# A causal rotary attention stage: weights above the diagonal zeroed by GpSimd, value tails projected in the setup, split f16 outputs

## The chip, the cores and the metric

One core of a Trainium2 chip runs the whole program. The metric is the device time of one execution, in microseconds (us). TensorE is written PE (its weight loads PEld), VectorE DVE, ScalarE ACT, GpSimd POOL and the queue that only issues DMAs SP. Each engine takes its instructions in order and waits on semaphores for the others.

## What is computed

The reference is a network of several parts over x of shape 8 x 512 x 256: a modulated dense layer with a landmark attention, an LSTM, a small attention with picked heads, an adaptive layer, a rotary attention, an RNN and a mixture of experts. The change touches the rotary attention alone:

```python
def _L1_attn_ref(x, norm_weight, w_qkv, w_out, persist_mem):
    h = rms_norm(x, norm_weight)
    q, k, v = jnp.split(h @ w_qkv.T, 3, axis=-1)      # 16 heads of 64
    q = apply_rope(q); k = apply_rope(k)
    k = jnp.concatenate([pm, k], axis=2)              # 4 memory rows ahead of 512 tokens
    v = jnp.concatenate([pm, v], axis=2)
    scores = jnp.einsum('bhid,bhjd->bhij', q, k) * scale
    causal = j <= i + (kv_len - n)
    attn = jax.nn.softmax(jnp.where(causal, scores, finfo.min), axis=-1)
    out = jnp.einsum('bhij,bhjd->bhid', attn, v)
    return out.reshape(b, n, heads * dim_head) @ w_out.T
```

## The kernel before

The program is a row of stages, each with a barrier behind it. attention_stage first loads the weights and splits each f32 chunk of w_qkv into a high f16 part (ACT) and a low f16 part (DVE). It then calls attention_core, which handles one pair of heads of one batch at a time: 8 batches x 8 pairs make 64 pairs. A product of f32 numbers is made of three f16 products (high by high, high by low, low by high), accumulated in PSUM.

attention_core is a software pipeline written out by hand. Every engine has a function rope_slot(it, s) that issues its share of slot s, and the order inside it is the order of the queue. In slot s, PE projects q and k of pair s+2 and the values of pair s+2, makes the maxima's scores of pair s+1 (scores), the transposed scores of pair s (scores_T for key tiles 0, 1 and 2, and 3 in the next slot) and weights times values of pair s-1 (values). The keys are 4 memory rows and 512 tokens, so tile 4 (called QT in the code) has only 4 keys, the "tail". A fifth key tile needs a value tail of 4 rows, which value_tail projects for each pair with 6 products.

The steps of one pair that matter here:

- rotate (DVE) reads a projection, turn and sum_up (POOL) finish the rotation, high (ACT) makes its f16 part in QK, low (POOL) the rest. In POOL's rope_slot the k of pair s+1 has its low part at the start of slot s, q of s+2 at the end.
- scores_T (PE) writes st_ps. It ends in the mask products of L861, which add -1e30 above the diagonal: a 128x128 bf16 identity by the matrix att_after.
- exps (ACT) makes the weights twice, PH in f16 (L1043) and P32 in f32 (L1048); low_weights (DVE, L979) makes PL = P32 - PH. values (PE, L874) waits for p_low.
- normalise (DVE, L991 and L993), turn_outputs (PE, L879) and keep_outputs (ACT, L1061) leave the pair's output in ao, in f32. After every eighth pair outputs (PE, L886) multiplies ao by wo in f32, and add_outputs (DVE, L997) adds the result to XT. Such a slot is called an output slot below.

ACT's order at the start of a slot, and POOL's whole order, are:

```python
                if s>=1: exps(it,s-1,2); exps(it,s-1,3)
                if s>=-1: keep_tail(it,s+1); high(it,2*(s+1)+1)
...
                if s>=-1: low(it,2*(s+1)+1); split_tail(it,s+1)
                turn(it,q); sum_up(it,q)
                if new_batch(s): low_tokens(it,s+3)
                turn(it,k)
                low(it,q)
                sum_up(it,k)
```

Of the kernel before, what the change touches and what calls it, by code (L numbers as in the profile page):

```python
# [5 lines left out]
P=128  # L6
# [727 lines left out]
def attention_core(nc, XT, HT, c_):  # L734
# [25 lines left out]
    with ExitStack() as ctx:  # L760
# [17 lines left out]
        v_done,v_hi,v_low,tail_done,tail_kept,tail_low=[sem(n) for n in "v_done,v_hi,v_low,tail_done,tail_kept,tail_low".split(",")]  # L778
# [3 lines left out]
        pe_passed=sem("pe_passed")  # L782
# [8 lines left out]
        def _(pe):  # L791
# [14 lines left out]
            def values_of(it,n,out,t,rows):  # L806
# [81 lines left out]
            def first_tail(it,n):  # L888
                if n: pe.wait_ge(tail_kept,n)
                value_tail(it,n)  # L890
            def rope_slot(it,s):
# [3 lines left out]
                elif s>=-1: first_tail(it,s+1)  # L895
# [41 lines left out]
        def _(dve):  # L937
# [3 lines left out]
            nc.vector.memset(PH[:,:,:],0.0).then_inc(cleared,1)  # L941
            nc.vector.memset(PL[:,:,:],0.0).then_inc(cleared,1)
# [1230 lines left out]
```

## Time and profile before

| what | value |
| --- | --- |
| time of the kernel, median of 3 runs | 4001.85 us (4001.58 to 4002.23) |
| the profiled execution's own time | 3965.16 us |
| its span | 3963.4 us |
| busy over the span: PE, DVE, ACT, POOL | 83%, 57%, 43%, 30% |
| the rotary attention's setup | from 2148.6 us |
| its first PE product, and the last slot's end | 2189.7 us, about 3220 us |

Times of rows are microseconds from the span's start. A row of the timeline gives start, duration, engine, line, operation, the tiles written and read, the shape, how many instructions were merged, and in brackets how long the engine sat idle before it and what released it. A matmul's record is longer than the time that it keeps the engine, because matmuls are pipelined: the time that a group takes is read from its start to the start of the next group. An f32 matmul leaves two records.

### The profile page before, as it was taken

Reading aid. Unit: us, or ns where it says so; the run is one execution under the profiler, and the core shown is the slowest. Engines: PE = TensorE matmul, PEld = TensorE weight load, DVE = VectorE, ACT = ScalarE, POOL = GpSimd, SP = SyncE. Lnnn points to the kernel's source line nnn. Section 1 sums busy time; section 2 is a strip of 40 time slices with the busy share of each in tenths; the row PEclk is TensorE's granted clock in tenths of the full one; section 3 lists DMA queues with packets and bytes.
Section 4 is the critical chain, followed back from the end, with each engine's and each line's share of the span. In section 5 each row is a group of like instructions: output and inputs, shape, how many; then the busy total and the mean of one; then the engine's idle time right before and its main releaser. Section 6 shows DMA issues by size and latency. Waiting matters only on the chain. (4 is left out here: it accounts for less than half of the span.)

```text
span 3963.4 us, 142208 instructions
## 1 busy us (share of the span) xinstructions
PE 3296.6 (83%) x58228; PEld 2450.2 (62%) x58228; DVE 2267.9 (57%) x6676; ACT 1694.8 (43%) x5249; POOL 1201.1 (30%) x1587
## 2 busy tenths in 40 slices
PE   5667759898888888559984899999999979999682
PEld 4455448888888888535531466666666647777561
DVE  4437754444444444368865777877779755555333
ACT  0129633333333333247742455655556534444231
POOL 0012330000000000023320555554555554444432
PEclk8789955555555555589997899999999975555686
DMA  3001010000000000011101000000000010101335
GB/s 119 8 26 54 19 42 24 14 14 24 14 24 14 24 14 24 5 33 24 24 0 49 2 2 2 2 2 2 2 2 2 2 45 31 35 31 35 87 118 170
DMA packets 111064, 115.69 MB, mean 29 GB/s; under 512 B 53132, under 2 KB 94549, under 8 KB 110458
## 3 DMA queue, kind: packets, MB, share of 16 engines
q1 hardware_dynamic: 102762, 87.07, 7.8%
q0 software_dynamic: 7824, 21.46, 1.5%
q8 instruction: 396, 6.49, 0.7%
q14 instruction: 82, 0.67, 0.1%
HBM read 79.49 MB, written 29.00 MB: 27 GB/s over the span
## 5 line engine op out<-in xcount | busy, mean ns | idle before, releaser
L649 PE MATMUL banks<-hp,whp 128*128 128x8 f16 x24576 | 741.3, 168 | 117.5 <-DVE hp L716 117.5
L649 PEld LDWEIGHTS banks<-hp,whp 128*128 128x128 f16 x24576 | 697.7, 104 | 178.3 <-DVE hp L716 169.4
L682 ACT ACTIVATE ig<-banks 128x32 f32<-128x32 f32 x512 | 101.2, 198 | 577.5 <-PE banks L649 577.5
L1043 ACT ACTIVATE att_PH<-att_stp 128x1024 f16<-128x1024 f32 (+3 forms) x258 | 183.4, 711 | 374.0 <-PE att_stp L861 374.0
L711 DVE SCALAR_TENSOR_TENSOR carry<-ig 128x16 f32<-128x16 f32 x512 | 92.2, 180 | 425.3 <-ACT ig L682 425.3
L619 POOL COPY HT<-hist 128x128 f32 x64 | 21.2, 406 | 986.6 <-DVE hp L721 986.6
L1659 PEld LDWEIGHTS rnn_banks<-rnn_hp,rnn_whp 128*128 128x128 f16 x6144 | 251.8, 108 | 102.3 <-ACT rnn_hp L1717 70.9
L1659 PE MATMUL rnn_banks<-rnn_hp,rnn_whp 128*128 128x8 f16 x6144 | 285.5, 171 | 35.3 <-ACT rnn_hp L1717 11.2
L1108 POOL TENSOR_TENSOR att_QK<-att_rot,att_QK 128x512 f16<-128x512 f32 x133 | 173.6, 1305 | 338.5 <-ACT att_QK L1035 338.5
L627 PE MATMUL banks<-xs,wxp 128*128 128x64 f16 x3168 | 264.9, 241 | 0.0
L979 DVE TENSOR_TENSOR att_PL<-att_P,att_PH 128x1024 f16<-128x1024 f32 (+3 forms) x257 | 235.1, 934 | 18.1 <-ACT att_P L1049 16.5
L804 PE MATMUL att_pj<-att_hT,att_w 128*128 128x512 f16 x804 | 199.2, 384 | 49.9 <-POOL att_hT L1116 48.4
L962 DVE TENSOR_REDUCE att_mx<-att_sp 128x2 f32<-128x264 f32 (+3 forms) x263 | 210.6, 822 | 30.3 <-PE att_sp L835 30.3
L1811 DVE TENSOR_TENSOR rnn_hp<-rnn_hist,rnn_hp 128x16 f16<-128x16 f32 x512 | 100.3, 196 | 204.0 <-ACT rnn_hist L1718 199.1
L1717 ACT ACTIVATE rnn_hp<-rnn_banks 128x16 f16<-128x16 f32 x512 | 94.2, 184 | 268.9 <-PE rnn_banks L1659 266.9
L1099 POOL TENSOR_TENSOR att_ab<-att_ab,att_rope 128x512 f32<-128x512 f32 x134 | 169.2, 1263 | 113.5 <-DVE att_ab L952 113.5
L627 PEld LDWEIGHTS banks<-xs,wxp 128*128 128x128 f16 x3168 | 195.7, 127 | 0.0
L1048 ACT ACTIVATE att_P<-att_stp 128x1024 f32<-128x1024 f32 (+3 forms) x258 | 180.5, 700 | 4.2 <-DVE att_PL L979 4.2
L874 PE MATMUL att_acc<-att_V,att_PH 128*128 128x65 f16 (+1 forms) x3584 | 179.8, 193 | 0.0
L874 PE MATMUL att_acc<-att_V,att_PL 128*128 128x65 f16 x1792 | 174.9, 192 | 0.0
L1103 POOL TENSOR_TENSOR att_rot<-att_ab 128x512 f32<-128x512 f32 x134 | 170.2, 1271 | 14.8
L716 DVE TENSOR_TENSOR hp<-og,tc 128x16 f16<-128x16 f32 x512 | 90.0, 176 | 144.3 <-ACT tc L688 144.3
(572 smaller groups left out, 7910.8 us busy)
## 6 DMA issues: line engine op xcount, KB each, us to landing
gen_w<-in_L_cond_W_dram SPq DMA_DIRECT2D x32, 512.0 KB, 4.2
exp_xt<-expert_rows_scratch SPq DMA_DIRECT2D x80, 129.0 KB, 2.3
edge_cb<-cols_scratch SPq DMA_DIRECT2D x16, 512.0 KB, 3.7
XT<-expert_found_scratch SPq DMA_DIRECT2D x16, 512.0 KB, 5.1
mod_xn<-in_x_dram SPq DMA_DIRECT2D x8, 512.0 KB, 3.7
XT<-in_xT_dram SPq DMA_DIRECT2D x1, 4096.0 KB
out_dram<-exp_ob SPq DMA_DIRECT2D x64, 64.0 KB, 2.2
attw_st<-in_L_attn_w_qkvT_dram SPq DMA_DIRECT2D x6, 512.0 KB, 4.4
```

Of the source, the lines that this page charges most:

```text
L627: last=nc.tensor.matmul(out, wxp[:,wpart,k,col:col+128], xs[:,st,xpart,k,steps], start=False,stop=False,skip_group_check=True)
L649: last=nc.tensor.matmul(out, whp[:,wpart,k,col:col+128], hp[:,k,hpart], start=False,stop=True,skip_group_check=True)
L804: last=nc.tensor.matmul(pj[:,:],c_.w_of(n)[:,wpart,k,col:col+P],h_of(n)[:,xpart,k,PM:PM+T],start=(i==0),stop=(i==5)); i+=1
L874: last=nc.tensor.matmul(out[:,0:wide],p[:,h,at:at+P],V[:,n%4,tt,part,h,0:wide],start=(tt==0 and a==0 and p is PH and part==0),stop=(tt==(R ...
L962: i=nc.vector.tensor_reduce(out=mx[:,:,qt:qt+1],in_=s_ps[:,:,at:at+w_],axis=X_AX,op=ALU.max); at+=w_
L979: i=nc.vector.tensor_tensor(PL[:,:,at:at+w_],P32[:,t%2,:,0:w_],PH[:,:,at:at+w_],ALU.subtract)
L1043: nc.scalar.activation(PH[:,:,at:at+w_],st_ps[:,:,0:w_],ACT.Exp,scale=DH**-0.5)
L1048: i=nc.scalar.activation(P32[:,t%2,:,0:w_],st_ps[:,:,0:w_],ACT.Exp,scale=DH**-0.5)
L1099: nc.gpsimd.tensor_tensor(ab[:,1],ab[:,1],c_.tab[:,1],ALU.mult).then_inc(turned,1)
L1103: nc.gpsimd.tensor_tensor(rot_of(j),ab[:,0],ab[:,1],ALU.add).then_inc(summed,1)
L1108: nc.gpsimd.tensor_tensor(dst[:,1],rot_of(j),dst[:,0],ALU.subtract).then_inc(lo,1)
L1659: last=nc.tensor.matmul(pre(st,par)[:,u,j], whp[:,wpart,k,u*P:u*P+P], hp[:,k,hpart], start=False,stop=True,skip_group_check=True)
```

## The change

- The mask products L861 leave scores_T. In their place POOL's new mask_weights sets the weights above the diagonal to zero, in PH and PL together, which now lie in one tile PHL: one affine_select over 128 partitions x 4 x 128 f16 for each key tile (t), and one more of 4 x 4 x 4 for the tail. values waits for its semaphore masked instead of p_low. POOL's slot order gets four such steps: for pair s-1 and t=1 first, then the low part of k, then t=2 and t=3, and at the slot's end pair s and t=0.
- value_tail, keep_tail and split_tail leave the loop. The setup projects the last 4 tokens of all batches at once, splits them and stores them in DRAM; SP fetches the 4 rows of a pair into V, in the loop.
- The memory values (pmv) enter with one product of 36 rows instead of two of 4.
- ao and wo are kept as two f16 parts. keep_outputs writes the high part, the new low_outputs (DVE) the low part, and outputs makes three f16 products for each f32 one. The value bank vo is free again after low_outputs.
- PE projects the values of pair s+2 after the third group of scores instead of before it.
- The setup loads all six chunks of w_qkv without waiting for a buffer; ACT and DVE also split wo there.

The diff, cut to what the text speaks of:

```diff
-        PH=sb("PH",[P,2,PCOLS],F16); PL=sb("PL",[P,2,PCOLS],F16); P32=sb("P32",[P,2,2,PM+T])
-        ao=sb("ao",[P,NP_,T]); o32=sb("o32",[P,QT,2,DH]); inv=sb("inv",[P,2,QT])
-        tail=sb("tail",[PM,2,DH]) if rope else None
+        PHL=sb("PHL",[P,2,2,PCOLS],F16); PH=PHL[:,0]; PL=PHL[:,1]; P32=sb("P32",[P,2,2,PM+T])
+        ao=sb("ao",[P,NP_,2,T],F16) if rope else sb("ao",[P,NP_,T]); o32=sb("o32",[P,QT,2,DH]); inv=sb("inv",[P,2,QT])
         mx=sb("mx",[P,2,5]); mparts=sb("mparts",[P,QT,P],BF16)
...
                 if rope and t==0:
-                    for part in range(2):
-                        last=nc.tensor.matmul(out,c_.identh[:,:],c_.pmv[:,n%NP_,part],start=False,stop=(part==1),skip_group_check=True)
+                    last=nc.tensor.matmul(out,c_.identh[:,:],c_.pmv[:,n%NP_],start=False,stop=True,skip_group_check=True)
...
-                elif n>2: pe.wait_ge(o_kept,it*S+n-2)
+                elif n>2: pe.wait_ge(o_low if rope else o_kept,it*S+n-2)
...
-            def value_tail(it,n):
-                values_of(it,n,st_ps[0:PM,0,T-P:T],QT,PM).then_inc(tail_done,1)
...
-                    if rope: pe.wait_ge(tail_kept,it*S+n+2)
...
-                if rope and t==QT-1: value_tail(it,n+2)
...
-                        for h in range(2): last=nc.tensor.matmul(st_ps[0:rows,h,at:at+w_],k_[head(h),kpart,tt*P:tt*P+rows],q[head(h),qpart,q0:T],start=False,stop=(i==2 and not rope),skip_group_check=True)
-                    if rope:
-                        d0=PM if tt==0 else 0; d1=PM if tt==QT else P
-                        for h in range(2): last=nc.tensor.matmul(st_ps[0:rows,h,at:at+d1-d0],c_.after[:,0:rows],c_.identb[:,d0:d1],start=False,stop=True,skip_group_check=True)
+                        for h in range(2): last=nc.tensor.matmul(st_ps[0:rows,h,at:at+w_],k_[head(h),kpart,tt*P:tt*P+rows],q[head(h),qpart,q0:T],start=False,stop=(i==2),skip_group_check=True)
                 last.then_inc(st_done,1)
...
-                pe.wait_ge(p_low,it*S*QT+n*QT+t+1)
+                pe.wait_ge(masked if rope else p_low,it*S*QT+n*QT+t+1)
...
-                if rope and t==QT-1: pe.wait_ge(tail_low,it*S+n+1)
+                if rope and t==QT-1: pe.wait_ge(tail_in[n%4],16*(it*(S//4)+n//4+1))
...
-                    last=nc.tensor.matmul((pj,vo)[m][:,:],c_.wo[:,q,m*P:(m+1)*P],ao[:,q,:],start=(q==0),stop=(q==NP_-1))
+                    if rope:
+                        for i,(wpart,opart) in enumerate(((0,0),(1,0),(0,1))):
+                            last=nc.tensor.matmul((pj,vo)[m][:,:],c_.wo[:,wpart,q,m*P:(m+1)*P],ao[:,q,opart,:],start=(q==0 and i==0),stop=(q==NP_-1 and i==2))
+                    else: last=nc.tensor.matmul((pj,vo)[m][:,:],c_.wo[:,q,m*P:(m+1)*P],ao[:,q,:],start=(q==0),stop=(q==NP_-1))
...
+                if s>=-1: scores(it,s+1,2)
                 if not after_outputs(s+2): project_values(it,s+2)
-                if s>=-1: scores(it,s+1,2)
...
+            def low_outputs(it,n):
+                dve.wait_ge(o_kept,it*S+n+1)
+                nc.vector.tensor_tensor(ao[:,n%NP_,1,:],vo[:,:],ao[:,n%NP_,0,:],ALU.subtract).then_inc(o_low,1)
...
                 if s>=-1: maxima(it,s+1,1)
+                if s>=1: low_outputs(it,s-1)
                 if out: add_outputs(it,s-1,0)
...
+                def tail_rows(b,n):
+                    rows=c_.tails[bass.ds(b,1),:,n%NP_].rearrange("a m part h d -> (a m) part h d")
+                    sp.dma_start(V[0:PM,n%4,QT,:,:,0:DH],rows).then_inc(tail_in[n%4],16)
+                for n in range(4): tail_rows(0,n)
+                with loop(nc,sp,NB//BPI) as it:
+                    for n in range(4,S+4):
+                        sp.wait_ge(pv_done,it*S*QT+(n-3)*QT)
+                        tail_rows(batch(it,n),n)
+                for i in range(4): sp.wait_ge(tail_in[i],16*(NB*NP_//4+1))
...
-            def keep_tail(it,n):
-                act.wait_ge(tail_done,it*S+n+1)
-                if n: act.wait_ge(tail_low,it*S+n)
-                nc.scalar.activation(V[0:PM,n%4,QT,0,:,0:DH],by_head(st_ps[0:PM,0,T-P:T]),ACT.Copy)
-                nc.scalar.activation(tail[:,:,:],by_head(st_ps[0:PM,0,T-P:T]),ACT.Copy).then_inc(tail_kept,1)
...
-                if s>=-1: keep_tail(it,s+1); high(it,2*(s+1)+1)
+                if s>=-1: high(it,2*(s+1)+1)
...
-            def split_tail(it,n):
...
+            def mask_weights(it,n,t):
+                pool.wait_ge(p_low,it*S*QT+n*QT+t+1)
+                pool.sem_inc(pool_passed,1)
+                for tt in ([t,QT] if t==QT-1 else [t]):
+                    d0=PM if tt==0 else 0; wide=(PM if tt==QT else P)-d0; rows=PM if tt==QT else P; at=written(tt)
+                    w=PHL[0:rows,:,:,at:at+wide].rearrange("p a h q -> p (a h) q")
+                    i=nc.gpsimd.affine_select(out=w,in_=w,compare_op=ALU.is_ge,fill=0.0,base=d0,pattern=[[0,4],[1,wide]],channel_multiplier=-1)
+                i.then_inc(masked,1)
...
-                if s>=-1: low(it,2*(s+1)+1); split_tail(it,s+1)
+                if s>=1: mask_weights(it,s-1,1)
+                if s>=-1: low(it,2*(s+1)+1)
+                if s>=1: mask_weights(it,s-1,2); mask_weights(it,s-1,3)
                 turn(it,q); sum_up(it,q)
                 if new_batch(s): low_tokens(it,s+3)
                 turn(it,k)
                 low(it,q)
                 sum_up(it,k)
+                if s>=0: mask_weights(it,s,0)
             def flat_slot(it,s):
...
+        wo=sb("wo",[P,2,PAIRS,D],F16); tab=sb("rope",[P,2,T]); pmk=sb("pmk",[P,PAIRS,2,PM],F16); pmv=sb("pmv",[PMR,PAIRS,P],F16)
...
+                for c in ORDER:
+                    sp.dma_start(st[:,c],w_qkvT[:,c*512:(c+1)*512].rearrange("(k p) n -> p k n",p=P)).then_inc(ld[c],16)
+                sp.dma_start(pk32[:,:,:],pmT).then_inc(ldk,16)
+                for r in (0,32): sp.dma_start(pv32[r:r+PM,:,:],pmV.rearrange("m n h d -> m n (h d)")).then_inc(ldk,16)
+                sp.dma_start(wo32[:,:,:],w_outT.rearrange("(a p) n -> p a n",p=P)).then_inc(wo_in,16)
+                sp.dma_start(tab[:,:,:],rope).then_inc(tab_in,16)
+                sp.wait_ge(kept_hi,2)
+                rows=tails.rearrange("b m n part h d -> (b m) n part (h d)")
+                sp.dma_start(rows[:,:,0],kept[:,0].rearrange("p (n e) -> p n e",e=P)).then_inc(written,16)
+                sp.wait_ge(kept_lo,2)
+                sp.dma_start(rows[:,:,1],kept[:,1].rearrange("p (n e) -> p n e",e=P)).then_inc(written,16)
+                sp.wait_ge(tab_in,16)
...
+                pe.wait_ge(last_tokens,3)
+                for j in range(2):
+                    pe.wait_ge(lo,j+1)
+                    i=0; col=2*INNER_+j*512
+                    for k in range(2):
+                        for wpart,xpart in ((0,0),(1,0),(0,1)):
+                            m=nc.tensor.matmul(ps[:,j],last[:,xpart,k],w[:,wpart,k,col:col+512],start=(i==0),stop=(i==5)); i+=1
+                    m.then_inc(projected,1)
...
+                    if i in (2,3):
+                        act.wait_ge(projected,i-1)
+                        nc.scalar.activation(kept[:,0,(i-2)*512:(i-1)*512],ps[:,i-2],ACT.Copy).then_inc(kept_hi,1)
+                act.wait_ge(wo_in,16)
+                nc.scalar.activation(wo[:,0],wo32[:,:,:],ACT.Copy).then_inc(wo_hi,1)
...
+                        at=slice((i-2)*512,(i-1)*512)
+                        nc.vector.tensor_tensor(kept[:,1,at],ps[:,i-2],kept[:,0,at],ALU.subtract).then_inc(kept_lo,1)
...
+                dve.wait_ge(wo_hi,1)
+                nc.vector.tensor_tensor(wo[:,1],wo32[:,:,:],wo[:,0],ALU.subtract).then_inc(pmh,1)
```

## Rows read from the trace of the kernel before

**Rows 1.** Windows: engines' busy us in one slot, TensorE's granted clock, DMA

```profile
2601.86:2615.71 13.85, 13.85 (x213) 8.96 (x210) 11.26 (x21) 8.12 (x18) 6.74 (x6) 1.00 0.01 2
```

**Rows 2.** One line's instructions, L991: duration min/median/max, first and last start

```profile
L991 DVE RECIPROCAL att_inv<-att_acc x64: 207/208/209, 2229.4 to 3198.9; 128x8 f32<-128x8 f32 x64
```

**Rows 3.** Timeline of PE, one ordinary slot

```profile
2603.26 0.39 PE L856 MATMUL att_stp<-att_mT,att_ones 64*128 64x512 bf16 x2
...
2604.23 0.28 PE L861 MATMUL att_stp<-att_identb,att_after 128*128 128x124 bf16 x2
2604.45 0.23 PE L832 MATMUL att_sp<-att_QK 64*128 64x132 f16 x2
...
2606.47 0.60 PE L879 MATMUL att_vo<-ident,att_o 128*128 128x128 f32 x4
...
2612.97 0.50 PE L810 MATMUL att_stp<-att_w,att_hT 128*4 128x128 f16 x6
2613.40 0.23 PE L856 MATMUL att_stp<-att_mT,att_ones 64*128 64x132 bf16 x2
...
2614.25 0.23 PE L874 MATMUL att_acc<-att_V,att_PH 128*128 128x65 f16 x2
```

**Rows 4.** Timeline of ACT, the same slot

```profile
2610.23 0.63 ACT L1035 ACTIVATE att_QK<-att_rot 128x512 f16<-128x512 f32 x1
...
2614.36 0.39 ACT L1043 ACTIVATE att_PH<-att_stp 128x264 f16<-128x264 f32 x1 [1.47 <-PE att_stp L861]
...
2615.44 0.61 ACT L1035 ACTIVATE att_QK<-att_rot 128x512 f16<-128x512 f32 x1
```

**Rows 5.** Timeline of POOL, the same slot

```profile
2610.94 1.42 POOL L1108 TENSOR_TENSOR att_QK<-att_rot,att_QK 128x512 f16<-128x512 f32 x1 [1.58 <-ACT att_QK L1035]
2612.43 1.26 POOL L1103 TENSOR_TENSOR att_rot<-att_ab 128x512 f32<-128x512 f32 x1
2616.13 1.16 POOL L1108 TENSOR_TENSOR att_QK<-att_rot,att_QK 128x512 f16<-128x512 f32 x1 [2.44 <-ACT att_QK L1035]
```

**Rows 6.** Timeline of DVE, the same slot

```profile
2608.85 2.50 DVE L979 TENSOR_TENSOR att_PL<-att_P,att_PH 128x1024 f16<-128x1024 f32 x2
...
2612.52 1.20 DVE L969 TENSOR_TENSOR att_mx<-att_mx 128x2 f32<-128x2 f32 x1
```

**Rows 7.** Timeline of POOL and DVE in the LSTM stage

```profile
1203.73 0.40 POOL L606 COPY xf<-XT 128x128 f32 x1
1203.74 0.42 DVE L719 TENSOR_TENSOR hist<-og,tc 128x16 f32<-128x16 f32 x1
```

**Rows 8.** One line's instructions, L719: duration ns min/median/max

```profile
L719 DVE TENSOR_TENSOR hist<-og,tc x512: 167/168/420, 552.9 to 1646.6; 128x16 f32<-128x16 f32 x171
```

**Rows 9.** Groups by form: busy us, mean ns, idle us before

```profile
L1187 POOL TENSOR_SCALAR_AFFINE_SELECT att_after<-att_after 128x128 bf16<-128x128 bf16 x1 | 0.3, 292 | 0.2 <-POOL att_after L1185 0.2
L2048 POOL TENSOR_SCALAR_AFFINE_SELECT adapt_mask<-adapt_mask 64x8 f32<-64x8 f32 x1 | 0.2, 185 | 0.1
L1244 POOL IOTA pick_heads_i<- 128x512 int32 x1 | 0.7, 671 | 0.0
...
L979 DVE TENSOR_TENSOR att_PL<-att_P,att_PH 128x520 f16<-128x520 f32 x64 | 44.8, 701 | 1.1 <-issue 1.1
L986 DVE TENSOR_TENSOR att_V<-att_vo,att_V 128x512 f16<-128x512 f32 x66 | 45.0, 682 | 2.1 <-ACT att_V L1053 1.1
```

**Rows 10.** Timeline of PE in an output slot

```profile
2337.27 3.65 PE L886 MATMUL att_vo<-att_ao,att_wo 128*128 128x512 f32 x8
2340.76 3.60 PE L886 MATMUL att_pj<-att_ao,att_wo 128*128 128x512 f32 x8
```

**Rows 11.** Timeline of the setup, SP and DVE

```profile
2148.61 0.38 SPq L1155 DMA_DIRECT2D attw_st<-in_L_attn_w_qkvT_dram  x1
...
2177.37 1.23 DVE L1179 TENSOR_TENSOR att_w<-attw_st,att_w 128x1024 f16<-128x1024 f32 x1 [1.50 <-ACT att_w L1166]
```

**Rows 12.** DMA view from 2140 to 2200 us, 40 slices of 1.5 us

```profile
GB/s 0 0 0 0 0 5 55 348 361 331 371 265 37 3 0 0 60 343 277 19 61 289 164 184 0 0 5 0 0 0 0 0 0 0 0 0 0 0 0 0
```

More of the change, by code:

```diff
@@ L777, in attention_core @@
         h_hi,h_ready,cleared,proj,evac,turned,summed,hi,lo,pm_kept=[sem(n) for n in "h_hi,h_ready,cleared,proj,evac,turned,summed,hi,lo,pm_kept".split(",")]
-        v_done,v_hi,v_low,tail_done,tail_kept,tail_low=[sem(n) for n in "v_done,v_hi,v_low,tail_done,tail_kept,tail_low".split(",")]
+        v_done,v_hi,v_low,o_low=[sem(n) for n in "v_done,v_hi,v_low,o_low".split(",")]
+        tail_in=[sem(f"tail_in{i}") for i in range(4)] if rope else None
         s_done,maxed,m_step,m_ready,m_turned,m_copied=[sem(n) for n in "s_done,maxed,m_step,m_ready,m_turned,m_copied".split(",")]
@@ L872, in values @@
                             at=weights_at(tt,a); out=acc[:,h,a*(DH+1):(a+1)*(DH+1)]
-                            for p,part,wide in ((PH,0,DH+1),(PH,1,DH),(PL,0,DH+1)):
-                                last=nc.tensor.matmul(out[:,0:wide],p[:,h,at:at+P],V[:,n%4,tt,part,h,0:wide],start=(tt==0 and a==0 and p is PH and part==0),stop=(tt==(ROWS-1) and p is PL),skip_group_check=True)
+                            for low,part,wide in ((0,0,DH+1),(0,1,DH),(1,0,DH+1)):
+                                last=nc.tensor.matmul(out[:,0:wide],PHL[:,low,h,at:at+P],V[:,n%4,tt,part,h,0:wide],start=(tt==0 and a==0 and low==0 and part==0),stop=(tt==(ROWS-1) and low==1),skip_group_check=True)
                 last.then_inc(pv_done,1)
@@ L1025, in _ @@
             slots(rope_slot if rope else flat_slot,dve)
-        if not rope: c_.select(nc,block,ctx,hi)
+        if rope:
+            @block.sync
+            def _(sp):
+                sp.wait_ge(cleared,6)
+                def tail_rows(b,n):
[7 more added lines that the diff above has]
+                for i in range(4): sp.wait_ge(tail_in[i],16*(NB*NP_//4+1))
+        else: c_.select(nc,block,ctx,hi)
         @block.scalar
@@ L1133, in _, with attention_stage @@
             slots(rope_slot if rope else flat_slot,pool)
-def attention_stage(nc, XT, HT, w_qkvT, w_outT, pmT, pmV, rope, ident):
+def attention_stage(nc, XT, HT, w_qkvT, w_outT, pmT, pmV, rope, ident, tails):
     with ExitStack() as ctx:
@@ L1162, in _ @@
             @block.scalar
             def _(act):
-                for c in range(NCH):
-                    act.wait_ge(ld[c%2],16*(c//2+1))
-                    nc.scalar.activation(w[:,0,:,c*512:(c+1)*512],st[:,c%2],ACT.Copy).then_inc(hi,1)
+                for i,c in enumerate(ORDER):
+                    act.wait_ge(ld[c],16)
+                    nc.scalar.activation(w[:,0,:,c*512:(c+1)*512],st[:,c],ACT.Copy).then_inc(hi,1)
+                    if i in (2,3):
+                        act.wait_ge(projected,i-1)
+                        nc.scalar.activation(kept[:,0,(i-2)*512:(i-1)*512],ps[:,i-2],ACT.Copy).then_inc(kept_hi,1)
@@ new lines, in _ @@
+                dve.wait_ge(last_tokens,1)
+                nc.vector.tensor_copy(last[:,0],low_last[:,:,:]).then_inc(last_tokens,1)
+                dve.wait_ge(last_tokens,2)
+                nc.vector.tensor_tensor(last[:,1],low_last[:,:,:],last[:,0],ALU.subtract).then_inc(last_tokens,1)
+                nc.vector.tensor_copy(identb[:,:],ident[:,:]).then_inc(pmh,1)
+                nc.vector.memset(pmv[:,:,:],0.0).then_inc(pmh,1)
+                for i,c in enumerate(ORDER):
+                    dve.wait_ge(hi,i+1)
+                    nc.vector.tensor_tensor(w[:,1,:,c*512:(c+1)*512],st[:,c],w[:,0,:,c*512:(c+1)*512],ALU.subtract).then_inc(lo,1)
+                    if i in (2,3):
+                        dve.wait_ge(kept_hi,i-1)
+                        at=slice((i-2)*512,(i-1)*512)
+                        nc.vector.tensor_tensor(kept[:,1,at],ps[:,i-2],kept[:,0,at],ALU.subtract).then_inc(kept_lo,1)
@@ L1188, in _ @@
                 step(nc.gpsimd.memset(ones[:,:],1.0))
+                step(nc.gpsimd.memset(identh[:,:],0.0))
+                for r in (0,32):
+                    step(nc.gpsimd.affine_select(out=identh[r:r+PM,:],in_=identh[r:r+PM,:],compare_op=ALU.not_equal,fill=1.0,base=0,pattern=[[-1,P]],channel_multiplier=1))
         c=Core(); c.pairs=PAIRS; c.rope=True; c.pm=PM; c.w=w; c.wo=wo; c.tab=tab; c.pmk=pmk; c.pmv=pmv; c.after=after; c.ones=ones; c.identb=identb; c.identh=identh; c.ident=ident; c.name='att'
+        c.tails=tails
         c.batch_per_turn=BPI_ATT; c.h_buffers=BPI_ATT; c.w_of=lambda n: w
```

62 lines of the change are left out of this document (26 added, 36 removed).

## The prediction

> **What bounds the kernel now.** The windows by stage come first, since the change touches one stage: the rotary attention, 2148.6 to about 3220 us. In an ordinary slot PE is busy for all of 13.85 us at a granted clock of 1.00 (2.4 GHz), DVE for 11.26, ACT for 8.12 and POOL for 6.74 [rows 1]. So PE sets the slot. L991 runs once a slot; its 64 starts lie 969.5 us apart [rows 2], 15.39 us a slot. With 56 intervals of 13.85 and 7 across an output slot, that makes 27.7 us for each of the latter. Then come the timelines of the same slot, engine by engine: the reader is to see where PE is in its order when the other engines deliver. POOL is idle half the time, but it does the low part of k late: scores_T of tile 3 ends at 2614.25 on PE [rows 3], ACT makes the last weights from 2614.36 and only then the high part of k, from 2615.44 [rows 4], and POOL can take the low part from 2616.13, for 1.16 us [rows 5]. Today nobody on PE waits for that before the next slot.
>
> **The change, part by part.**
>
> *PE gives back 1.6 us a slot.* The value tail took 2612.97 to 2613.40, 0.43. scores_T of tile 0 took 2603.26 to 2604.45, 1.19, of which 0.22 is its mask [rows 3]; without the mask PE stays on 64-row products and need not switch to 128 rows and back, for which I take 0.10, so 0.32 go. scores_T of tile 3 with its tail took 0.85 (2613.40 to 2614.25): two masks and one switch go, about 0.43. Six products of 128 columns took 0.43 in the tail, 0.07 each; the masks of tiles 1 and 2 thus give 0.14 each, the merged memory product 0.07, and moving the value projection saves a switch, 0.10. The sum is 1.6. By itself that would be a slot of 12.25.
>
> *The outputs give back 3.7 us per output slot.* Eight f32 records, four products, took 3.49 and 3.53 us [rows 10], 0.88 each; 16 are 14.1 us. Three f16 products of 512 columns replace each, at four times the 0.054 of 128 columns net of issue, 0.217: 10.4 us. 8 x 3.7 = 30 us, less what the new waits take back (below).
>
> *low_outputs* costs DVE what low_values of the same shape costs, 0.68 [rows 9]. DVE would have 11.9 us a slot, under the 12.25, so it is no bound by its sum. It delays low_weights of tiles 0 and 1 behind it by 0.6. The value projection now waits for it and for the maxima that it was moved past, about 0.75 us of PE in a slot. Both are hidden if the slot is set elsewhere, as I hold it is.
>
> *The masks on POOL.* No row shows this size. The same operation takes 0.292 us for 128 elements a partition and 0.185 for 8 [rows 9]: 0.89 ns an element, 0.63 us for 512. The bounds are 0.29 (as if four rows cost one) and 1.17 (four times the small one); a generator of 512 elements took 0.67 [rows 9], near the first figure, so I take 0.63, 0.19 for the tail, and 0.07 to 0.10 between two POOL instructions that wait. POOL's sum rises from 6.74 to about 9 us: not a bound either. The place in the queue is what costs. In a slot POOL now does, without a pause: low of q, sum of k, mask 0, mask 1, low of k, mask 2, mask 3. values of tiles 2 and 3 wait for the last two; behind them on PE stand scores_T of tile 0, the scores and the projection of k, whose end starts the rotation that leads to low of q and sum of k again. That is a ring, and I add it up from the end of PE's projection of k:
>
> - to the end of POOL's sum of k: before, 2606.47 [rows 3] to 2613.69 (2612.43 + 1.26 [rows 5]), 7.2. low_weights of tile 1 ended there at 2611.35 [rows 6], and low of q ended 1.0 later. low_outputs puts that back by 0.6; the 0.4 that low_weights of tile 0 now loses to POOL goes. New: 7.4.
> - masks 0 and 1, low of k, masks 2 and 3 with the tail: 4 x 0.63 + 0.19 + 1.16, and five gaps: 4.3. low of k could not start before 8.75 in this count: scores_T of tile 3 ends at 7.2 (PE's 7.8 of before, less 1.35, plus the 0.75), and 1.88 of ACT follow it [rows 3 to 5], less 0.3 for the two tail copies. The first two masks end at 8.9, so the two conditions nearly meet.
> - DVE's operations that fall into this stretch and share POOL's port: 1.1 (next paragraph).
> - values of tile 3, 18 of the products of L874: 0.55.
> - scores_T of tile 0, the first scores and the projection of k: 2603.26 to 2606.47 less 0.32, 2.9.
>
> Sum 16.25; I forecast 16.2 us for an ordinary interval, 2.35 above today's 13.85. PE is then idle for some 4 us of it.
>
> *The port.* DVE's L969, two columns from SBUF, took 1.20 us beginning 0.09 after POOL's sum of k, and ended with it [rows 5, 6]; POOL's low of q took 1.42 instead of 1.16 while a low_weights ran. Whether an operation of POOL with one input does the same, the LSTM stage shows: a POOL copy from 1203.73 for 0.40 stretched a DVE operation with two SBUF inputs to 0.42, where the median is 0.168 [rows 7, 8]. So I take it that affine_select, which reads SBUF too, excludes DVE's two-input operations. L975, low_weights of tile 2 (0.70 [rows 9]) and of tile 3 (about 0.4, plus its tail) must run between the masks, and mask 3 depends on them: 1.1 net of overlap.
>
> The Trainium skill ("SBUF — State Buffer", Who interferes with whom) says the same in general: a DVE instruction with two SBUF inputs contends with a GpSimd instruction that reads SBUF, and the second to issue waits for the whole of the first. By it the ring is 16.2, without it 15.1; for affine_select itself no run here shows it. The skill's "GPSIMD Engine Reference" (Elementwise — side-by-side cycle accounting) gives for a tight loop about 1.8 cycles an element, 0.77 us for 512; by this estimate the ring would be 0.56 longer than with my slope from [rows 9].
>
> *What else waits.* Behind mask 3 on POOL stand turn and sum of q; DVE's rotation of k and ACT's high of q need them. They end at 12.8 + 2.7 = 15.5 in my count, before the projection of k ends (16.2). The fetch of a tail is issued three slots ahead and hidden; if that cover went, some 4 us would be added a slot, as a small load takes.
>
> *Output intervals.* They save 1.6 + 3.7, and give back the wait for low_outputs (1.2, nothing covers it there) and the stall before tiles 2 and 3 (about 1.8, since the value projection after an output slot covers 1.7 of it): 2.3 each, 18 us in 8.
>
> *Setup.* The last low part ends at 2178.6 today [rows 11]. The queue reached 331 to 371 GB/s when it had work [rows 12]. All 4.75 MB then land 13.6 us after 2150.5, the chunk of wo at about 2163. ACT needs two pieces of 1.06 for it and DVE two of 1.23; DVE's own list (six chunks 7.4, memory rows about 3, tails 1.5, wo 2.5) ends near 2169.5. The tails' two stores lie under that. Gain 9 us (5 to 12).
>
> **Sum.** 56 x 2.35 = +132, outputs -18, setup -9: +105 us. The profiled execution took 3965.16 us for a span of 3963.4; the median of the runs is 36.7 us above it, and I add the difference to the median: 4001.85 + 105 = 4107.
>
> **Rivals.**
> - *The masks don't lose the port.* Ring 15.1, output intervals 3.3 saved: 56 x 1.25 - 26 - 9 = +35, 4037. For it: no row shows affine_select beside DVE. Against: [rows 7].
> - *Masks at a bound.* At 0.29 each and no port loss low of k waits for ACT, the interval is 14.35 and the sum 28 - 28 - 9, -9: 3993. At 1.17 each the ring is 18.4 and the time about 4230.
> - *Faster: the masks are short enough to fit in POOL's idle time.* With no cost for them the chain through low of k alone gives 13.9 and -35, 3967. The sides change at an interval of 14.5, a mask of about 0.35 without port loss. If some slack that I don't see lets PE remain the bound, with slots of 12.3 to 13, the sum is near -110, 3890. For it: POOL is half idle and PE full [rows 1]. Against: POOL's idle time lies before low of k [rows 5], where masks 2 and 3 can't be.
> - *The clock.* PE would be busy for three quarters of a slot; if its granted clock fell to 0.5, PE's part of the ring doubles, several us a slot, over 4300. Its pauses are under 3 us, so I give it little.
>
> **How the numbers follow.** My forecast (intervals 15.6 to 16.8, 4070 to 4150) has 0.50; no port loss or cheaper masks but still slower 0.25; dearer masks or the clock 0.07; a small result within 0.2% 0.05; faster 0.13. 0.2% is 8 us, about what a measurement of this kernel can tell from no change. The range 4015 to 4150 takes in the case without port loss and leaves out the faster cases and the dear masks.
>
> **What the profile after would show.** L991 at intervals of 16.2; PE idle before L874's tiles 2 and 3, released by POOL's PHL, 2 to 3 us a slot; 320 affine_selects, 256 of about 0.63; DVE's L975 and small low_weights lengthened beside them; DVE's new subtraction at 0.68; L886's work down to 10.4 us an output slot; the setup done near 2169; a clock of 1.00. An interval under 14.5, or PE waiting for DVE instead of POOL, would make the prediction wrong, and so would a mask far from 0.63.

## The result, and the profile after

The changed kernel took 4072.97 us (median of 4 runs, 4070.12 to 4076.09) against 4002.04 us: a ratio of 1.0175, 95% interval 1.0158 to 1.0193. It is 71 us slower, where 105 were forecast; 4073 lies in the range of 4015 to 4150.

The two spans differ by more, 4068.4 - 3963.4 = 105 us. A second profile of the kernel before (experiment e0 below) has a span of 4003.2 us and the same ordinary slot. Against that one the difference of 65 us falls apart as in the table. The expert stage runs there from the first load of exp_xt to the start of its last write-back (L1932 before, L1982 after):

| part | before, second profile | after | difference |
| --- | --- | --- | --- |
| all ahead of the attention's setup | 2152.8 | 2154.8 | +2.0 |
| setup, first DMA issue to the core's first memset | 30.7 | 21.6 | -9.1 |
| attention core, to the RNN's first instruction | 1045.4 | 1123.8 | +78.4 |
| RNN and dispatch | 497.9 | 493.5 | -4.4 |
| expert stage | 218.5 | 217.1 | -1.4 |
| from there to the end of the span | 57.9 | 57.6 | -0.3 |

The page after, its busy line and slices:

```profile
PE 3230.3 (79%) x57260; PEld 2395.4 (59%) x57260; DVE 2396.8 (59%) x6745; ACT 1675.2 (41%) x5120; POOL 1387.5 (34%) x1845
...
PE   5667758888888888389895888888888879999572
...
PEclk8789955555555555599997999999999975555686
```

Each slice is 102 us. The attention fills slices 22 to 31, counted from 0: PE falls there from 9 tenths or more to 8, and the clock stays at 9 tenths or more. The windows view of one ordinary slot comes next (stretch, its length, busy us of PE, PEld, DVE, ACT and POOL, the granted clock, the DMA share and GB/s), and then the line of the reciprocal, L981 now, which answers [rows 2]:

```profile
2631.02:2646.61 15.59, 13.02 (x191) 8.14 (x191) 14.53 (x23) 8.14 (x16) 10.95 (x12) 1.00 0.00 1
```

```profile
L981 DVE RECIPROCAL att_inv<-att_acc x64: 207/208/209, 2226.8 to 3279.3; 128x8 f32<-128x8 f32 x64
```

The ordinary interval is 15.59 us instead of 13.85. 63 intervals make 1052.5 us; read from the single starts, the 56 ordinary ones are 15.61 on average and the seven across an output slot 25.5 instead of 27.7. The granted clock in the slot is 1.00. PE in this slot, the groups around its waits (they answer [rows 3]):

```profile
2633.80 0.60 PE L871 MATMUL att_vo<-ident,att_o 128*128 128x128 f32 x4
...
2636.31 0.39 PE L829 MATMUL att_sp<-att_QK 64*128 64x512 f16 x2 [0.42 <-DVE att_mx L953]
...
2641.85 1.62 PE L866 MATMUL att_acc<-att_V,att_PHL 128*128 128x65 f16 x48 [0.70 <-POOL att_PHL L1121]
2643.31 0.39 PE L841 MATMUL att_sp<-att_identb,att_mparts 128*128 128x128 bf16 x4
2644.88 0.72 PE L866 MATMUL att_acc<-att_V,att_PHL 128*128 128x65 f16 x18 [1.19 <-POOL att_PHL L1121]
2645.86 0.72 PE L866 MATMUL att_acc<-att_V,att_PHL 128*128 128x65 f16 x18 [0.26 <-POOL att_PHL L1121]
2646.51 0.39 PE L851 MATMUL att_stp<-att_mT,att_ones 64*128 64x512 bf16 x2
```

The reader is to see the brackets: before values of tile 0 (0.70 us), of tile 2 (1.19) and of tile 3 (0.26) PE sat idle until POOL's L1121, the affine_select. With the 0.42 for DVE's maxima that is all of its idle time in the slot. POOL and DVE at the same time (they answer [rows 5] and [rows 6]):

```profile
2638.05 1.82 POOL L1109 TENSOR_TENSOR att_QK<-att_rot,att_QK 128x512 f16<-128x512 f32 x1 [1.38 <-ACT att_QK L1042]
2639.95 1.26 POOL L1104 TENSOR_TENSOR att_rot<-att_ab 128x512 f32<-128x512 f32 x1
2641.17 1.22 POOL L1121 TENSOR_SCALAR_AFFINE_SELECT att_PHL<-att_PHL 128x496 f16<-128x496 f16 x2
2642.65 1.39 POOL L1109 TENSOR_TENSOR att_QK<-att_rot,att_QK 128x512 f16<-128x512 f32 x1 [0.27 <-ACT att_QK L1042]
2644.00 0.83 POOL L1121 TENSOR_SCALAR_AFFINE_SELECT att_PHL<-att_PHL 128x512 f16<-128x512 f16 x1
2645.00 0.80 POOL L1121 TENSOR_SCALAR_AFFINE_SELECT att_PHL<-att_PHL 128x512 f16<-128x512 f16 x2 [0.18 <-DVE att_PHL L972]
```

```profile
2640.03 1.21 DVE L959 TENSOR_TENSOR att_mx<-att_mx 128x2 f32<-128x2 f32 x1
2641.27 0.57 DVE L963 TENSOR_SCALAR att_mparts<-att_mx 128x8 bf16<-128x8 f32 x1
2641.87 0.57 DVE L965 SCALAR_TENSOR_TENSOR att_mparts<-att_mx,att_mparts 128x8 bf16<-128x8 f32 x1
2642.34 1.99 DVE L969 TENSOR_TENSOR att_PHL<-att_P,att_PHL 128x520 f16<-128x520 f32 x2
2644.25 0.58 DVE L972 TENSOR_TENSOR att_PHL<-att_P,att_PHL 4x8 f16<-4x8 f32 x1
```

POOL runs the seven steps of the ring with hardly a pause, masks 0 and 1 merged in one row. DVE's small operations are held up beside them, by the port as I read it: L963 and L965 take 0.57 each. The groups by form from 2400 to 3100 us give their mean, before (L973, L975) and then after:

```profile
L975 DVE SCALAR_TENSOR_TENSOR att_mparts<-att_mx,att_mparts 128x8 bf16<-128x8 f32 x45 | 8.8, 195 | 1.6
L973 DVE TENSOR_SCALAR att_mparts<-att_mx 128x8 bf16<-128x8 f32 x45 | 8.3, 185 | 1.6
```

```profile
L1121 POOL TENSOR_SCALAR_AFFINE_SELECT att_PHL<-att_PHL 128x496 f16<-128x496 f16 x42 | 26.2, 623 | 41.4 <-DVE att_PHL L969 41.4
...
L969 DVE TENSOR_TENSOR att_PHL<-att_P,att_PHL 128x264 f16<-128x264 f32 x42 | 53.3, 1269 | 0.0
...
L972 DVE TENSOR_TENSOR att_PHL<-att_P,att_PHL 4x8 f16<-4x8 f32 x42 | 24.4, 582 | 0.0
L963 DVE TENSOR_SCALAR att_mparts<-att_mx 128x8 bf16<-128x8 f32 x42 | 23.8, 567 | 1.5
L965 DVE SCALAR_TENSOR_TENSOR att_mparts<-att_mx,att_mparts 128x8 bf16<-128x8 f32 x42 | 22.7, 542 | 1.4
```

### The profile page after: what moved, and what is told of

It reads as the page before. It is cut to its first block and busy times, and to the rows that moved or that the text cites. A ratio compares the mean times of both kernels' runs of the same rounds, so it can differ in the third digit from the quotient of the medians.

```text
span 4068.4 us, 141073 instructions
## 1 busy us (share of the span) xinstructions
PE 3230.3 (79%) x57260; PEld 2395.4 (59%) x57260; DVE 2396.8 (59%) x6745; ACT 1675.2 (41%) x5120; POOL 1387.5 (34%) x1845
## 5 line engine op out<-in xcount | busy, mean ns | idle before, releaser
L1050 ACT ACTIVATE att_PHL<-att_stp 128x1024 f16<-128x1024 f32 (+3 forms) x258 | 183.2, 710 | 419.6 <-PE att_stp L853 419.6
L1709 PE MATMUL rnn_banks<-rnn_hp,rnn_whp 128*128 128x8 f16 x6144 | 286.1, 171 | 37.8 <-ACT rnn_hp L1767 13.9
L866 PE MATMUL att_acc<-att_V,att_PHL 128*128 128x65 f16 (+1 forms) x5376 | 195.5, 193 | 131.2 <-POOL att_PHL L1121 131.2
L866 PEld LDWEIGHTS att_acc<-att_V,att_PHL 128*128 128x128 f16 x5376 | 172.8, 97 | 155.7 <-POOL att_PHL L1121 147.9
L969 DVE TENSOR_TENSOR att_PHL<-att_P,att_PHL 128x1024 f16<-128x1024 f32 (+3 forms) x257 | 260.9, 1053 | 0.5 <-issue 0.2
L1109 POOL TENSOR_TENSOR att_QK<-att_rot,att_QK 128x512 f16<-128x512 f32 x133 | 204.6, 1539 | 109.6 <-ACT att_QK L1042 109.6
L1121 POOL TENSOR_SCALAR_AFFINE_SELECT att_PHL<-att_PHL 128x512 f16<-128x512 f16 (+2 forms) x321 | 181.7, 582 | 92.3 <-DVE att_PHL L969 81.1
L1104 POOL TENSOR_TENSOR att_rot<-att_ab 128x512 f32<-128x512 f32 x134 | 170.3, 1271 | 15.1
```

The costliest lines, as they stand in the source:

```text
L866: last=nc.tensor.matmul(out[:,0:wide],PHL[:,low,h,at:at+P],V[:,n%4,tt,part,h,0:wide],start=(tt==0 and a==0 and low==0 and part==0),stop=(t ...
L969: i=nc.vector.tensor_tensor(PL[:,:,at:at+w_],P32[:,t%2,:,0:w_],PH[:,:,at:at+w_],ALU.subtract)
L1050: nc.scalar.activation(PH[:,:,at:at+w_],st_ps[:,:,0:w_],ACT.Exp,scale=DH**-0.5)
L1104: nc.gpsimd.tensor_tensor(rot_of(j),ab[:,0],ab[:,1],ALU.add).then_inc(summed,1)
L1109: nc.gpsimd.tensor_tensor(dst[:,1],rot_of(j),dst[:,0],ALU.subtract).then_inc(lo,1)
L1121: i=nc.gpsimd.affine_select(out=w,in_=w,compare_op=ALU.is_ge,fill=0.0,base=d0,pattern=[[0,4],[1,wide]],channel_multiplier=-1)
```

## The experiments

All but e0 start from the changed kernel. "Interval" is the distance of two ordinary starts of the reciprocal in the experiment's own profile. "Ratio" is to the kernel before, timed beside that experiment, with its 95% interval in brackets.

### e0: the kernel before, profiled again

> The kernel before once more, unchanged, for a second profile of it. The profiled execution of before took 3965 us, while its timed runs took 4001 to 4006 (now 3994 to 4008 in 11 runs), and the expert stage lasted 192 us in it, but 217 to 223 us in the profiles of the changed kernel and of the four experiments so far. Theory: that one execution had a short expert stage by chance, and a second profile shows 215 to 223 us there, the same ordinary interval of 13.85 us, and a span near 4000. Rival: the expert stage of the kernel before is really shorter, 192 us again, and the change lengthened it by 25 us from afar.

Span 4003.2 us, time 4004.97 (a single run); interval 13.85; expert stage 218.5 us. The profiles of all eleven changed versions have 214 to 223 us there too. The first profile's 192 us in that stage was an accident of that execution, and the change is not charged with it. The interval of 13.85, on which the forecast stood, is the same in both.

### e1: the low part of k behind the masks

```diff
-                if s>=1: mask_weights(it,s-1,1)
-                if s>=-1: low(it,2*(s+1)+1)
-                if s>=1: mask_weights(it,s-1,2); mask_weights(it,s-1,3)
+                if s>=1: mask_weights(it,s-1,1); mask_weights(it,s-1,2); mask_weights(it,s-1,3)
+                if s>=-1: low(it,2*(s+1)+1)
```

> The changed kernel with one line of POOL's order moved: masks 1, 2 and 3 first, then the low part of k. Theory (the ring through POOL's queue): values of tiles 2 and 3 no longer wait behind the 1.2 to 1.4 us of the low part of k and behind ACT's high part, so the ordinary interval falls from 15.59 us to about 14.8 (masks 0 and 1 still come late) and the time by about 45 us, to 4028, ratio to the kernel before 1.006. Rival (the masks' own durations and their port set the slot, wherever they stand): interval stays at 15.3 to 15.6, time over 4055.

Time 4016.39, ratio 1.0035 (1.0024 to 1.0045); interval 14.77. POOL's timeline, one slot:

```profile
2630.75 1.27 POOL L1104 TENSOR_TENSOR att_rot<-att_ab 128x512 f32<-128x512 f32 x1
2631.98 1.22 POOL L1121 TENSOR_SCALAR_AFFINE_SELECT att_PHL<-att_PHL 128x496 f16<-128x496 f16 x2
2634.00 0.68 POOL L1121 TENSOR_SCALAR_AFFINE_SELECT att_PHL<-att_PHL 128x512 f16<-128x512 f16 x1 [0.80 <-DVE att_PHL L969]
2634.85 0.81 POOL L1121 TENSOR_SCALAR_AFFINE_SELECT att_PHL<-att_PHL 128x512 f16<-128x512 f16 x2 [0.17 <-DVE att_PHL L972]
2635.64 1.15 POOL L1109 TENSOR_TENSOR att_QK<-att_rot,att_QK 128x512 f16<-128x512 f32 x1
```

From the end of the sum of k to the end of mask 3 it is now 3.6 us (2632.02 to 2635.66) instead of 4.6. Two swapped lines give back 57 of the 71 us, 12 more than expected; the intervals across output slots fell too, from 25.5 to 24.7. What is left in the ring shows in the bracket of mask 2: it waits 0.80 for DVE's L969, which comes late because L963 and L965 ahead of it took 0.57 and 0.56 beside masks 0 and 1, instead of 0.19 and 0.20.

### e2: no masking at all

The three lines that call mask_weights are gone, and values waits for p_low in place of masked.

> The changed kernel without any masking: no operation on POOL and no product on PE, values waits for the low part again, so weights above the diagonal stay in the output. Theory: with the ring gone PE sets the slot, 12.25 us of its own work and about 0.75 us of waits for the maxima and low_outputs: interval 12.9 to 13.1, time about 4002 + 56 x (13.0 - 13.85) - 8 x 3.9 - 10 = 3913, ratio 0.978. Rival (the vo bank, held until low_outputs, or DVE's sum is what lengthens the slot): interval 14.5 or more, ratio above 1.00.

Time 3932.7, ratio 0.9819 (0.980 to 0.9839); interval 13.02, some at 14.0. One slot's windows:

```profile
2617.20:2630.22 13.02, 12.60 (x191) 8.08 (x191) 12.40 (x23) 8.14 (x17) 8.03 (x6) 1.00 0.01 3
```

PE sets the slot again, though not by much: it is busy for 12.60 of the 13.02, DVE for 12.40. So the masks on POOL cost 2.6 us a slot, and neither the vo bank nor DVE's sum does. The time came out 20 us above the expected 3913; 13 of it are the ordinary intervals, 13.24 on average over all 56.

### e3: masks that only write

```diff
-                    i=nc.gpsimd.affine_select(out=w,in_=w,compare_op=ALU.is_ge,fill=0.0,base=d0,pattern=[[0,4],[1,wide]],channel_multiplier=-1)
+                    i=nc.gpsimd.memset(w,1.0)
```

> The changed kernel with each affine_select replaced by a memset of the same columns to 1.0, so that the masked blocks are all ones in the output: POOL keeps its place and its waits, but only writes. Theory with the port (reading POOL work excludes DVE's two-input work): memset of 512 takes 0.52 instead of 0.62 and DVE's L965 and L969 are no longer stretched beside it, the interval falls to about 14.9, of which 0.4 is the shorter operation. Rival (the port costs nothing here): 15.2.

Time 4027.02, ratio 1.0055 (1.0036 to 1.0074); interval 14.90. The groups by form show what the port does:

```profile
L963 DVE TENSOR_SCALAR att_mparts<-att_mx 128x8 bf16<-128x8 f32 x44 | 36.9, 839 | 1.5
...
L965 DVE SCALAR_TENSOR_TENSOR att_mparts<-att_mx,att_mparts 128x8 bf16<-128x8 f32 x44 | 10.3, 234 | 1.5
L972 DVE TENSOR_TENSOR att_PHL<-att_P,att_PHL 4x8 f16<-4x8 f32 x44 | 6.5, 148 | 0.0
```

L972, with two SBUF inputs, is short again, 0.148 instead of 0.582, and it runs inside the memset of mask 2. L965 is short as well, 0.234 instead of 0.542, but shows nothing: L963 ahead of it, with one input, is held until both memsets have ended, and L965 has none beside it. POOL and then DVE in one slot:

```profile
2628.39 0.98 POOL L1121 MEMSET att_PHL<- 128x496 f16 x2
2631.21 1.14 POOL L1121 MEMSET att_PHL<- 128x512 f16 x3
...
2628.51 0.90 DVE L963 TENSOR_SCALAR att_mparts<-att_mx 128x8 bf16<-128x8 f32 x1
2629.45 0.20 DVE L965 SCALAR_TENSOR_TENSOR att_mparts<-att_mx,att_mparts 128x8 bf16<-128x8 f32 x1
...
2631.48 0.15 DVE L972 TENSOR_TENSOR att_PHL<-att_P,att_PHL 4x8 f16<-4x8 f32 x1
```

So a POOL operation that only writes leaves the two-input L972 alone, and one that reads doesn't. L963 and L965 together take as long as in the changed kernel, 1.10 against 1.14. The memset itself took 0.524 us, 0.1 less than the select; four of them are 0.4 of the 0.69 us that the interval fell, and the port's share is at most the other 0.3.

### e4: the mask products back on PE

As e2, with the products of L861 restored behind the three products of scores_T; tails in the setup, split outputs and the later value projection stay.

> The changed kernel with the mask products on PE again and nothing masked on POOL; tails in the setup, split outputs and the later value projection stay. Theory: PE sets the slot with 13.85 less 0.43 for the tail and 0.06 for the memory product, plus up to 0.5 of waits for the maxima and low_outputs: interval 13.4 to 13.85, outputs save about 2.5 us eight times, setup 10: time 3945 to 3972, ratio 0.986 to 0.993. Rival (the split outputs or the late values are what made the kernel slower): ratio above 1.00.

Time 3966.4, ratio 0.991 (0.9891 to 0.993); interval 13.80. The rest of the change is a gain of 36 us; masking by POOL alone turned it into a loss. The two kernels differ by 107 us.

### e5: values projected ahead of the third scores again

On top of e4:

```diff
-                if s>=-1: scores(it,s+1,2)
                 if not after_outputs(s+2): project_values(it,s+2)
+                if s>=-1: scores(it,s+1,2)
```

> As e4_products_back (mask products on PE, no masks on POOL), and the value projection ahead of the third group of scores again. Theory: PE then waits at the value projection for low_outputs, about 1.0 us, instead of 0.4 and 0.2 at the scores and the projection, so the interval is 13.8 to 14.1, no shorter than the 13.80 of e4. Rival (moving the projection alone made e4 miss its 13.4): interval 13.4.

Time 3995.33, ratio 0.9979 (0.997 to 0.9988); interval 14.34, above the 13.8 to 14.1 of the theory. PE now waits at the value projection for low_outputs, 0.8 to 1.0 us a slot in the view of waits:

```profile
PEld att_vo L810 <- DVE att_ao L989: 37.0, 38, 1.0
PE att_vo L810 <- DVE att_ao L989: 30.5, 38, 0.8
```

So the move was worth 0.54 us a slot, given that low_outputs stands behind the maxima.

### e6: masks of 32 columns

```diff
-                    d0=PM if tt==0 else 0; wide=(PM if tt==QT else P)-d0; rows=PM if tt==QT else P; at=written(tt)
+                    d0=PM if tt==0 else 0; wide=(PM if tt==QT else P)-d0; rows=PM if tt==QT else P; at=written(tt); wide=min(wide,32)
```

> The changed kernel with masks of 32 columns instead of 128 (the rest of each masked block stays unmasked in the output): same places and waits in POOL's queue, about 0.29 us each instead of 0.62. Theory: all four stand in the ring, so the interval falls by nearly 4 x 0.33 = 1.3 us plus some of the port's share, until ACT's high part of k, 1.5 us after scores_T of tile 3, holds the low part: 14.2 to 14.4 us, time about 4000 to 4010. Rival (only the place in the queue counts): above 15.2.

Time 4001.89, ratio 0.9994 (0.9985 to 1.0004); interval 14.42. With masks half as long (0.306 us), which leave most of each block unmasked, the changed kernel is level with the kernel before: the duration counts too, at the same place in the queue.

### e7: products on PE, and low_outputs ahead of the second maxima

On top of e5:

```diff
-                if s>=-1: maxima(it,s+1,1)
                 if s>=1: low_outputs(it,s-1)
+                if s>=-1: maxima(it,s+1,1)
```

> As e5, and DVE's low_outputs ahead of the second group of maxima, so that vo is free when PE comes to the value projection and the maxima are done behind it. Theory: both waits of PE go, interval 13.35 to 13.45, time 20 to 27 us below e4, 3940 to 3947, ratio 0.985 to 0.986. Rival (keep_outputs on ACT or the two-input work of DVE comes too late and the wait moves on): interval 13.8 as before.

Time 3939.05, ratio 0.9829 (0.9816 to 0.9842); interval 13.40:

```profile
2606.76:2620.16 13.40, 13.40 (x201) 8.63 (x201) 12.41 (x24) 8.15 (x17) 7.85 (x7) 1.00 0.01 2
```

PE is busy for the whole slot. This version beats both kernels, the one before by 1.7% and the changed one by 134 us.

### e8: the same two moves with the masks on POOL

e7's orders on PE and DVE, masking as in the changed kernel.

> The changed kernel, masks on POOL in their place, with the two moves that made e7 faster than e4 (values projected ahead of the third scores, low_outputs ahead of the second maxima). Theory (the ring through POOL runs beside PE's waits for DVE, and only its longest branch counts): the 0.6 us of PE's waits that go shorten nothing, interval 15.5 to 15.7 as the changed kernel, time within 10 us of it. Rival (PE's waits add to the ring, as they do where PE sets the slot): interval 15.1 to 15.2, 25 us less.

Time 4057.9, ratio 1.0147 (1.0125 to 1.017); interval 15.60. The same moves that bring 0.40 us a slot over e4 bring nothing here: the ring through POOL hides PE's waits. POOL and then DVE, one slot, in which PE's projection of k ends at 2628.46:

```profile
2635.84 1.22 POOL L1121 TENSOR_SCALAR_AFFINE_SELECT att_PHL<-att_PHL 128x496 f16<-128x496 f16 x2
2637.03 1.68 POOL L1109 TENSOR_TENSOR att_QK<-att_rot,att_QK 128x512 f16<-128x512 f32 x1
2638.66 0.83 POOL L1121 TENSOR_SCALAR_AFFINE_SELECT att_PHL<-att_PHL 128x512 f16<-128x512 f16 x1
...
2637.00 2.00 DVE L969 TENSOR_TENSOR att_PHL<-att_P,att_PHL 128x520 f16<-128x520 f32 x2
```

The low part of k no longer waits for ACT (0.27 in the changed kernel), but it lasts 1.68 instead of 1.39 and ends at the same place, 10.25 us behind the projection of k against 10.24. In both kernels L969 of tile 2 starts 8.54 us behind the projection of k, after L963 and L965. On these figures the branch that counts in the middle of the ring runs through DVE: masks 0 and 1 on POOL, L963 and L965 beside them, L969, and behind that the low part of k.

The time is 15 us below the changed kernel, more than the 10 expected. The kernel before was 3 us faster beside these runs (3998.94), and the intervals across output slots fell from 25.5 to 24.5, which is 8 us over eight of them.

### e9 and e10: is the shared port a floor?

e9 is e1 with the memset of e3; e10 is e1 with the moves of e8.

> e1 and e3 together: the low part of k behind the masks, and each affine_select replaced by a memset to 1.0 (the masked blocks are all ones in the output). Theory (in e1 the shared port is what is left: POOL's reading work, about 10 us a slot, and DVE's two-input work, about 3.9, sum to 13.9 of its 14.77): without the masks' 2.65 us on the port the sum is 11.3, and the interval falls to between 13.4 and 13.9, set by PE and its waits or by masks 0 and 1 behind the sum of k. Rival (e1 is set by the order alone): the memset brings as much as in e3 less the port's part, 14.77 - 0.4 = 14.4.

> e1 and e8 together: masks by affine_select, the low part of k behind them, and PE's waits for DVE gone. Theory (the port's sum of 13.9 us a slot is a floor for any order of this work): interval between 14.3 and 14.8, time no less than the kernel before. Rival (with a good order masks on POOL beat products on PE): interval below 13.85, down to the 13.0 of e2.

e9: 3970.23 us, ratio 0.9932 (0.9907 to 0.9956), interval 14.1. e10: 4004.7 us, ratio 1.0014 (1.0005 to 1.0024), interval 14.75 to 14.8. e10 is where the floor put it, but e1 was there already; e9 fell by 0.67 us against e1, as e3 did against the changed kernel (0.69), to a value between both expectations. It also shows the port from POOL's side. POOL and then DVE, one slot:

```profile
2631.85 1.04 POOL L1121 MEMSET att_PHL<- 128x512 f16 x3 [1.03 <-DVE att_PHL L969]
...
2630.99 1.04 DVE L969 TENSOR_TENSOR att_PHL<-att_P,att_PHL 128x520 f16<-128x520 f32 x2
2631.95 0.15 DVE L972 TENSOR_TENSOR att_PHL<-att_P,att_PHL 4x8 f16<-4x8 f32 x1
```

The memset of mask 2 starts inside the second L969, 0.19 us before its end, and neither is longer for it: the memsets of 512 take 0.52, and this L969 (128x264) 0.427, where it took 0.432 in the kernel before. In the changed kernel the select at this place starts inside the same L969 and takes 0.83 instead of 0.62. That the port's sum is a floor is not shown. What e10 shows is that two better orders don't bring masks on POOL under the 13.85 of the products.

## Why the prediction was right

The prediction's own terms against the profile after:

- **PE's own work, 12.25 us a slot.** e2 gives 12.60 busy, and 0.42 of waiting for the maxima: the change gave PE back 1.25 us and not 1.6. e7, with the products, has 13.40 and PE always busy, where the prediction's terms without the masks' part make 13.35. The miss didn't touch the forecast, in which PE doesn't set the slot; PE's idle time in a slot came out at 2.6 us instead of 4.
- **From the projection of k to the end of POOL's sum of k, 7.4.** 2633.80 to 2641.21: 7.41.
- **The mask at 0.63 us**, read as a slope from two small ones [rows 9]: 0.623. The figure of the Trainium skill ("GPSIMD Engine Reference", Elementwise — side-by-side cycle accounting), 1.8 cycles an element and so 0.77 us for 512 as an estimate, was not met.
- **Masks, low of k and the port, 4.3 + 1.1.** This is the term that was mis-sized: 2641.21 to 2645.80 is 4.6. The operations alone are 3.9, as in the sum; gaps and port together took 0.7, not 1.5. I gave every POOL instruction a gap of 0.07 to 0.10, and masks 0 and 1 ran with none. And I added DVE's two-input work at full length: its cost shows as 0.23 on the low of k (1.39 instead of 1.16), 0.2 on mask 2 (0.83 instead of 0.62) and the 0.18 in the bracket of mask 3, while the rest ran where POOL waited for ACT (0.27) or had work that didn't clash.
- **low of k not before 8.75, the first two masks done at 8.9.** It started at 8.85, released by ACT, and the masks were done at 8.6. The two conditions nearly met, as said, the other way round; by the figures of e8 the low part's end hung on L969 and not on either.
- **values of tile 3 and on to the projection of k, 0.55 + 2.9.** 2645.86 to 2646.51 is 0.65, and 2.89 follow (2630.91 to 2633.80 a slot earlier).
- **The ring, 16.2.** 15.6. The 0.6 us less, 56 times, are 33 of the 34 us by which the forecast was too high.
- **Output intervals -2.3 each.** -2.3, 27.7 to 25.5. Their products (L880) took 10.6 us, where 10.4 were forecast, and the wait for low_outputs 1.0, where 1.2 were. **Setup -9.** -9.1.
- **PE idle before tiles 2 and 3.** It was, for 1.45 us where 2 to 3 were forecast; another 0.70 came before tile 0, which the prediction didn't name.
- **PE's waits for DVE, hidden.** Shown by e8, and priced where they are not hidden by e4, e5 and e7: 0.40 a slot, 27 us in all.
- **The port.** The Trainium skill ("SBUF — State Buffer", Who interferes with whom) has it that reading POOL work holds up two-input DVE work and writing doesn't. The traces agree: L972 took 0.582 beside the select and 0.148 beside the memset (e3), and where POOL starts inside an L969 the select takes 0.83 and the memset its usual 0.52 (e9).
- **The rivals.** A clock falling to half didn't come, 1.00 in the slot. "No port loss" gave 4037 and 15.1; the truth lies half-way between it and the forecast. The range held both, so that the time alone doesn't decide between them. "Faster, since POOL has idle time" is refuted: the place costs, for e1 moves POOL's work without removing any and gets 57 us, and so does the amount, for e6 halves the masks in their place and gets 71.

Four slips of the text. The stretch of [rows 1] begins in the idle time ahead of the first slot behind an output slot, so that it misses a low of k on POOL and some of DVE. The next slot of the same view reads:

```profile
2617.22:2631.07 13.85, 13.85 (x208) 8.95 (x206) 12.31 (x23) 8.46 (x18) 7.97 (x8) 1.00 0.00 1
```

POOL's sum before was thus 8.0 and not 6.74; the conclusion, no bound by sum, stands (10.95 of 15.59 after). DVE's sum was 12.3 and not 11.26. With the 0.68 of low_outputs it makes 13.0, above the 12.25 of PE, so that "no bound by its sum" doesn't follow from these rows; e2, with DVE at 12.40 beside PE's 12.60, shows that it was close. In the changed kernel DVE is busy for 14.53 of the 15.59 us, the growth being low_outputs and operations that are held up. The chain through low of k "alone" is 13.4 by its own terms (8.75 + 1.16 + 0.55 + 2.9), not 13.9, which would have put that rival lower still. And the second gap of the fp32 products, 3.53 us, has no row of its own there.

The median moved by 71 and the forecast was made on one profile whose expert stage was short by 26 us. That didn't touch the forecast, since only differences inside the attention were used.

## What to carry to other kernels

An engine with half its time idle is no free place for work: ask where in its queue the new work stands, what the instruction ahead of it waits for, and whether the chain closes on the engine that now sets the pace. Add up that ring from rows before moving work; here it gave the interval within 4%. When a change bundles several parts, the sum of a good part and a bad one hides both: the mask products cost PE about 0.8 us a slot (13.40 in e7 against the 12.60 that PE is busy in e2), the masks on POOL 2.6, and the rest of the change was worth 36 us, or 63 with the two orders of e7.

## What the runs showed of the hardware that was not expected

- A tensor_scalar from f32 to bf16 of 8 columns, with one SBUF input, took 0.185 us before and on average 0.567 in the changed kernel, beside POOL's affine_select, and 0.839 in e3, beside POOL's memset. It is held up by a POOL operation that only writes, where the two-input L972 is not (4x8, 0.148 in e3). Beside two memsets in a row it waited for the end of the second (0.90 us, e3). The Trainium skill ("SBUF — State Buffer", Who interferes with whom) lists tensor_scalar among the operations that can take the pair of ports shared with GpSimd; the runs agree.
- affine_select over 128 partitions x 4 x 124 f16 takes 0.623 us, a memset of the same 496 elements 0.513: reading and comparing costs 0.1 us more than writing.
- One execution had an expert stage of 192 us where the twelve other profiles, of all versions, have 214 to 223. What shortened it is open.
